# A graph layer on one core: 80 half-target edge buckets in place of 40, chunk addresses loaded four at a time, plain groups out of PSUM by ScalarE, small edge tables partly on GpSimd

## The reference

```python
for r in range(weight.shape[0]):
    mask = (edge_type == r).astype(x.dtype)
    sums = jax.ops.segment_sum(msgs * mask[:, None], dst, num_segments=n)
    cnt = jax.ops.segment_sum(mask, dst, num_segments=n)
    mean = sums / jnp.maximum(cnt, 1.0)[:, None]
    out = out + mean @ weight[r]
```

## Time and profile before

| what | value |
|---|---|
| median of 3 runs | 1880.09 us |
| span of the profiled execution | 1878.8 us |
| PE busy | 1794.9 us (96%) |
| DVE busy | 1023.3 us (54%) |
| ACT busy | 478.5 us (25%) |
| POOL busy | 701.1 us (37%) |
| first stage, start to last histogram add | 0 to 427.5 us |

### The profile page before, as it was taken

How to read it: one execution, slowest core, us unless ns; L and a number is a source line. 1 busy time by engine, 2 the same in 40 slices (tenths; PEclk the granted TensorE clock), 3 DMA queues, 4 the chain that set the end, 5 groups by cost and what they waited for, 6 DMA issues and landing times.

```text
span 1878.8 us, 28666 instructions
## 1 busy us (share of the span) xinstructions
PE 1794.9 (96%) x9953; PEld 1477.4 (79%) x9953; DVE 1023.3 (54%) x2540; ACT 478.5 (25%) x1055; POOL 701.1 (37%) x609
## 2 busy tenths in 40 slices
PE   6999999999999999999999999954999999999999
PEld 4876689987777778787777887742899888878987
DVE  7888999997254543526354356786632224362311
ACT  3139956662010110101011145243100000111100
POOL 2110000003634435353534444200485552345862
PEclk9999999999999999999999999956999999999999
DMA  4532222224213121231313534110354351113322
GB/s 134 154 109 77 73 86 79 75 67 129 91 38 89 45 72 56 66 86 47 94 33 113 172 84 131 45 46 7 96 164 146 104 156 51 37 55 118 90 73 66
DMA packets 129282, 162.23 MB, mean 86 GB/s; under 512 B 14288, under 2 KB 75368, under 8 KB 128922
## 3 DMA queue, kind: packets, MB, share of 16 engines
q1 hardware_dynamic: 100848, 120.93, 21.5%
q10 hardware_dynamic: 22250, 23.53, 4.0%
q0 software_dynamic: 6080, 16.40, 2.9%
HBM read 135.51 MB, written 25.30 MB: 86 GB/s over the span
## 4 chain that ended last, share of the span: by engine, by line
PE 84%; DVE 6%; ACT 6%; issue 1%; DVEq 1%; DMA 1%; POOL 0%; ACTq 0%; SPq 0%
PE ps L367 22%; PE ps L368 22%; PE ps L369 21%; PE ps L1236 9%; PE ps L892 3%; ACT sc_col L838 2%; ACT sc_row L837 1%; PE ps L1201 1%; DVE w_lo L318 1%; PE ps L881 1%; PE ps L1156 1%; DMA nat<-in_x 1%; ACT w_hi L313 1%; PE ps L1183 1%; PE ps L1211 0%
## 5 line engine op out<-in xcount | busy, mean ns | idle before, releaser
L367 PE MATMUL ps<-w_hi,xt_hi 128*125 128x512 f32 x1320 | 539.0, 408 | 9.1 <-DVE xt_lo L549 3.5
L256 POOL TENSOR_TENSOR w_hi<-w_stage,zero 128x512 fp32r<-128x512 f32 x256 | 276.8, 1081 | 684.4 <-PE ps L369 670.0
L368 PE MATMUL ps<-w_lo,xt_hi 128*125 128x512 f32 x1320 | 523.0, 396 | 0.0
L369 PE MATMUL ps<-w_hi,xt_lo 128*125 128x512 f32 x1320 | 521.5, 395 | 0.0
L259 POOL TENSOR_TENSOR w_lo<-w_stage,w_hi 128x512 fp32r<-128x512 f32 x256 | 346.2, 1352 | 20.1
L367 PEld LDWEIGHTS ps<-w_hi,xt_hi 128*125 128x125 f32 x1320 | 246.6, 187 | 67.1 <-DVE xt_lo L549 4.3
L369 PEld LDWEIGHTS ps<-w_hi,xt_lo 128*125 128x125 f32 x1320 | 246.0, 186 | 63.3
L368 PEld LDWEIGHTS ps<-w_lo,xt_hi 128*125 128x125 f32 x1320 | 246.3, 187 | 53.5
L367 PE MATMUL ps<-xt_hi,w_hi 128*128 128x314 f32 x736 | 250.5, 340 | 1.3 <-DVE ring L2430 0.6
L369 PE MATMUL ps<-xt_hi,w_lo 128*128 128x314 f32 x736 | 225.9, 307 | 0.0
L368 PE MATMUL ps<-xt_lo,w_hi 128*128 128x314 f32 x736 | 225.7, 307 | 0.0
(11 more groups left out here) (392 smaller groups left out, 2390.2 us busy)
## 6 DMA issues: line engine op xcount, KB each, us to landing
w_stage<-in_stream SPq DMA_DIRECT2D x374, 256.0 KB, 2.7
pre<-ring POOLq DMA_DIRECT2D x30, 250.0 KB, 3.8
a_qt<-pre_t SPq DMA_DIRECT2D x18, 312.5 KB, 3.8
a_qt<-pre_t ACTq DMA_DIRECT2D x14, 312.5 KB
pre_t<-ring_t POOLq DMA_DIRECT2D x12, 312.5 KB, 2.8
pre_t<-ring_t ACTq DMA_DIRECT2D x12, 312.5 KB
a_vx<-pre SPq DMA_DIRECT2D x9, 312.5 KB
nat<-pre SPq DMA_DIRECT2D x2, 1250.0 KB
```

The source lines that it names most:

```text
L256: POOL.tensor_tensor(w_hi[:, q, :], w_stage[:, q % NST, :], zero[:].to_broadcast([128, 512]), ALU.add).then_inc(S("hi_done"), 1)
L367: PE.matmul(dst, l_hi, r_hi, start=first, stop=False)
L368: PE.matmul(dst, l_hi, r_lo, start=False, stop=False)
L369: return PE.matmul(dst, l_lo, r_hi, start=False, stop=last)
```

## The change

- **Buckets.** The key gets the half of the target (destination at or above 314): 80 buckets (NKEY) of 314 columns. A chunk of 128 edges, not a group of 256, belongs to one bucket; there are still 240 chunks, now 120 pairs. Per pair: 2 matmuls of 314 columns, each into its own bank (banks 4, 5 and 6, 7 in turn), one ACT copy of 2x314, and per chunk one hot column of 314 and one add of 314 int16. Hot rows are made four chunks at once by one tensor_tensor of 128x(128x4), float16. Hot tiles are made 4 chunks ahead (LEAD_HOT), in the order add(c), hot(c + 4), and each add also waits for the add before it. The idle slots of the first turned group are 1, 2 and every fourth from 7 to 35.
- **Addresses.** `g_start` holds each chunk's start in `adj`; four are loaded into registers by one call each four chunks.
- **Edge tables.** Three keys are packed as fields of one number in 28 rows (28x166 = 4648 elements in place of 6600), with one tensor_tensor more (`key_weight`), and later unpacked. GpSimd makes the field weights, a float16 key, and the column and row numbers (some 15 operations of 125x166). The positions' chunk starts are looked up by 80 tensor_scalar of 166 elements (one a key) into `key_start` and five halving adds of int16.
- **Plain groups 0 to 3** leave PSUM by ACT (copy without bias), each ahead of the last chunk split of its group. Their bias is added on DVE once they are read back, 125x2560 an operation: `bias_half(nat, 0)` and `(nat, 1)` around the feed steps of the projection, `bias_half(z, 0)` and `(z, 1)` ahead of the two clips (L1548). Four more transfers (SP) bring these biases.
- POOL's store and split loops stand later in the program's text; their order among themselves is as it was.

```diff
+SPLIT = 314
+NKEY = 2 * NBUCKET
+FIELDS, NROW = 3, 28
+CHUNK = 128
+NCHUNK = (EDGES + NKEY * (CHUNK - 1)) // CHUNK
+NPAIR = NCHUNK // 2
...
+        def evacuate_plain(g):
+            for m in range(T):
+                wait_bank(ALE, g, m, c0, g0)
+                if g:
+                    ALE.wait_ge(S(f"st{tag}_{m}"), 16 * g)
+                ALE.activation(ring[:, m, :], ps[0:P, m, :], ACT.Copy).then_inc(S("bank_free"), 1)
...
+        DVE.tensor_tensor(key_weight[:], key_hot[:], e_weight[:].unsqueeze(1).to_broadcast([P, NROW, EW]), ALU.mult)
...
+    def hist_add(c, start):
+
+        DVE.wait_ge(S("hi_main"), c // 2 + 1)
+        if c:
+            DVE.wait_ge(S("hi_add"), c)
+        o = adj[:, bass.ds(start, SPLIT)]
+        DVE.tensor_tensor(o, o, counts[c // 2 % 4][:, c % 2, :], ALU.add).then_inc(S("hi_add"), 1)
+
+    def hist_pe(g):
+
+        if g >= 2:
+            PE.wait_ge(S("hi_main"), g - 1)
+        if g == 1:
+            PE.wait_ge(S("bank_free"), (SC0 + SC_GROUPS + 1) * T)
         for j in range(2):
+            c = 2 * g + j
+            PE.wait_ge(S("hi_dve"), c + 1)
+            PE.matmul(ps[0:P, pair_bank(g) + j, 0:SPLIT], hot_row[c // 4 % 2][:, 0:P, c % 4], hot_col[c % 8][:],
+                      start=True, stop=True).then_inc(S("hi_pe"), 1)
...
         for g in range(3):
-            load_bias(g)
-            for c in range((g + 1) * KT, (g + 2) * KT):
+            for c in range((g + 1) * KT, (g + 2) * KT - 1):
                 split_act(c)
-        load_bias(3)
+            evacuate_plain(g)
+            split_act((g + 2) * KT - 1)
...
+        starts = dict(enumerate(hist_starts(0)))
         for h in range(HI_GROUPS):
             for n in range(per):
-                g = h * per + n
-                if g + 2 < NGROUP:
-                    hist_dve_hot(g + 2, (g + 2) % 4)
-                if chunk_at(h, n):
-                    split_dve(chunk_at(h, n))
-                if g % 4 == 0:
-                    packed = DVE.value_load(gpack[0:1, g // 4:g // 4 + 1], min_val=0, max_val=2 ** 24 - 1)
-                hist_dve_add(g, g % 4, packed)
+                for c in (2 * (h * per + n), 2 * (h * per + n) + 1):
+                    hist_add(c, starts[c])
+                    if c + LEAD_HOT < NCHUNK:
+                        hist_hot(c + LEAD_HOT)
+                    if c % STARTS == 0 and c + STARTS < NCHUNK:
+                        starts.update(zip(range(c + STARTS, c + 2 * STARTS), hist_starts(c + STARTS)))
+                    if c % 2 == 0 and chunk_at(h, n):
+                        split_dve(chunk_at(h, n))
...
     DVE.tensor_copy(dis[:], rs[:])
+    DVE.wait_ge(S("ld_bh"), 32)
+    bias_half(nat, 0)
     for k in range(5, KT):
         feed_dve(k, k)
+        if k == 6:
+            bias_half(nat, 1)
...
     DVE.drain().then_inc(S("rgam"), 1)
+    DVE.wait_ge(S("ld_z"), 32)
+    DVE.wait_ge(S("ld_bh"), 64)
+    for g in range(2):
+        bias_half(z, g)
     for i, w in enumerate((w1, w2)):
         DVE.wait_ge(S("w_round"), i + 1)
```

More of the change, by code:

```diff
@@ L498, in dense @@
                 dense_pe(g, c0, g0, between=between)
-        side(dense, evacuate, evacuate_half, load_bias)
+        side(dense, evacuate_plain, evacuate, evacuate_half, load_bias)
         stored(groups - 2)
@@ L727, in bucket_counts @@
-        evacuate(0)
+        DVE.scalar_tensor_tensor(e_key[:], e_key[:], 2.0, e_half[:], ALU.mult, ALU.add)
+        DVE.drain()
+        row, first = e_row[:, 0:EC], e_first[:, 0:EC]
+        DVE.tensor_scalar(first, e_key[:], float(NROW), None, ALU.is_ge)
+        DVE.tensor_scalar(e_second[:], e_key[:], float(2 * NROW), None, ALU.is_ge)
+        edge_tables(sig(DVE.drain(), "dve_step"))
+        DVE.scalar_tensor_tensor(row, first, -float(NROW), e_key[:], ALU.mult, ALU.add)
+        DVE.drain()
@@ L895, in beside, with pair_bank, hist_hot @@
-    def beside(dense, evacuate, evacuate_half, load_bias):
-        mk = bucket_counts(evacuate)
+    LEAD_HOT, STARTS = 4, 4
+    def pair_bank(g):
+        return 4 if g % 2 else 6
+    def hist_hot(c):
+        if c % 4 == 0:
+            if c >= 8:
+                DVE.wait_ge(S("hi_pe"), c - 4)
+            DVE.tensor_tensor(hot_row[c // 4 % 2][:], iota1_by4[:],
+                              slot_row[:, c:c + 4].unsqueeze(1).to_broadcast([128, 128, 4]), ALU.is_equal)
+        if c >= 8:
+            DVE.wait_ge(S("hi_pe"), c - 7)
+        DVE.tensor_scalar(hot_col[c % 8][:], iota1_16[:, 0:SPLIT], slot_col[:, bass.ds(c, 1)], None,
+                          ALU.is_equal).then_inc(S("hi_dve"), 1)
@@ new lines, in hist_copy, with hist_starts @@
+    def hist_copy(g):
+        b = pair_bank(g)
+        ALE.wait_ge(S("hi_pe"), 2 * g + 2)
+        if g >= 4:
+            ALE.wait_ge(S("hi_add"), 2 * g - 6)
+        ALE.activation(counts[g % 4][:], ps[0:P, b:b + 2, 0:SPLIT], ACT.Copy).then_inc(S("hi_main"), 1)
+    def hist_starts(c):
+        top = (NBUCKET - 1) * NB + SPLIT
+        return nc.values_load_multi_w_load_instructions(
+            g_start[0:1, c:c + STARTS], engines=(mybir.EngineType.DVE,), min_val=0, max_val=top,
+            skip_runtime_bounds_check_because="a bucket's number is below NKEY")[1]
@@ L975, in beside, with idle @@
                 DVE.wait_ge(S("sc_pe"), sc_per + EC + 1)
[L976 removed]
+                DVE.tensor_copy(slot_col[:], slot_ps[:, 0:NCHUNK])
+                DVE.tensor_copy(slot_row[:], slot_ps[:, NCHUNK:2 * NCHUNK])
                 DVE.drain()
[L978 to L979 removed]
+                for c in range(LEAD_HOT):
+                    hist_hot(c)
             evacuate(i + SC0)
[L982 to L983 removed]
         HI0 = SC0 + SC_GROUPS
         assert HI0 + HI_GROUPS == G_PRE0
[L986 to L987 removed]
+        per = NPAIR // HI_GROUPS
+        assert per * HI_GROUPS == NPAIR and per * 4 == KT * T * 3
+        def idle(h, s_):
+            return s_ in (1, 2) or s_ > 2 and s_ % 4 == 3 and 3 < s_ < 36 if h == 0 else s_ % (4 if h < HI_GROUPS - 1 else 8) == (
+                3 if h < HI_GROUPS - 1 else 7)
         def hist_of(h, s_):
[L990 to L992 removed]
+            n = sum(not idle(h, i) for i in range(s_))
+            return n if not idle(h, s_) and n < per else None
         def first_step(h, k):
@@ L1093, in build, with load_bias_h @@
     load_rounds(C_REL + 2 * NSL, C_PROJ - NSL, KT * G_PROJ)
+    def load_bias_h(row):
+        for g in range(2):
+            r = B_PRE0 + row + g
+            SP.dma_start(bias_h[g][:], a["bias"][r:r + 1, :].rearrange("o (k f) -> o k f", k=4).to_broadcast([P, 4, 128])).then_inc(S("ld_bh"), 16)
     def sp_late(c):
```

355 lines of the change are left out of this document (190 added, 165 removed).

## The result

The changed kernel takes 1885.35 us, the median of ten runs (1882.55 to 1887.32); the kernel before took 1879.99 in ten runs beside it (1879.24 to 1880.39). The ratio is 1.0028, with a 95% interval of 1.0019 to 1.0037. It is slower by 5.4 us, where I had forecast 1.0 us faster, a change too small to be measured. The time lies in the stated range. The spread of the changed kernel is four times that of the kernel before.

What follows compares the result with a forecast made beforehand. The histogram was taken as bound by DVE and PE together. Tables 0.8, before the histogram -0.4, projection biases 0, histogram -5.0 and z biases 3.6 gave -1.0: 1879.1 us, own range 1872 to 1886, with rivals 1858 to 1893.

Steps and rivals of the forecast that it cites:

- tables, to the first scatter tile: Edge tables: DVE's end covered, but ACT evacuates group 3 behind zeroing `adj`; +0.8 us, bounds -0.5 and +6.
- from there to the first add: Before the histogram: DVE makes the first four hot tiles in 1.2 for 1.84, copies slots in two steps; -0.4 us.
- first add to the end: Histogram: a column group takes 44.2 us against 45.8, one more window at the end +1.4; -5.0 us in all.
- gate, z biases: Gate: two bias operations run from 1139.0 to 1144.6 ahead of the clips, which start 3.6 late without cover; +3.6 us.
- upper bound of +5.6: Gate: the most that the z biases were taken to cost, in us; the lower bound was 0.
- rival 1: Histogram: latency is hidden and the loop goes by its load, 38.3 to 42 a group; 1850 to 1866 us, chance 0.26.
- address loads: Histogram on DVE: loading four addresses takes 0.13 us each time, x 7.5 = 1.0 a column group; 0 to 0.6 possible.
- 32 us of idle time before the adds: Histogram on DVE: idle time before the add's line, about 0.27 a pair, ended by ACT's copy.
- Rival 2: Histogram: the loop is slower than before, add waiting for ACT's copy, 49 a group; 1891 to 1897 us, chance 0.16.
- Rival 3: Edge tables: 80 lookups at 0.3 make them late, PE stands around 100 to 130 us; 1884 to 1888, chance 0.10.
- Rival 4: Gate: the z biases cost nothing because their transfers are early; -3.6, 1875.5 us, chance 0.08.
- the signs: Forecast wrong if a histogram column group is under 43 or over 46 us, or if PE stands before 140 us.

Runs made afterwards that it cites:

- x3_b2: The kernel before with two operations of 125x2560 on z (its maximum with itself) ahead of the clips, without bias transfers: 1883.93 us.
- x1_early: The changed kernel with the two z bias transfers issued by SP five chunks earlier: 1884.35 us.
- x8_static: The changed kernel with each add at a fixed address and no address loads (counts go to wrong buckets): 1878.90 us, one run.
- x9_nochain: As x8_static, but each add waits for the add 8 chunks before, not for the last one: 1876.13 us, one run.
- x6_ev3: The changed kernel with the z biases moved behind the clips and group 3 taken out of PSUM by DVE, lead 4: 1871.44 us, one run.
- x7_lead6: As x6_ev3, with hot tiles made 6 chunks ahead of their add, not 4: 1863.75 us.
- x11_lead8: As x7_lead6, with a lead of 8 chunks, 12 hot columns and three tiles of hot rows: 1859.13 us.
- x4_b4: The kernel before with four operations of 125x2560 on z ahead of the clips: 1890.20 us.

## Why the prediction was wrong

Step by step, profile against profile:

| step | forecast | measured |
|---|---|---|
| tables, to the first scatter tile | +0.8 | +1.7 (143.50 for 141.82) |
| from there to the first add | -0.4 | -2.0 (101.80 for 103.81) |
| first add to the end | -5.0 | -3.6 (178.25 for 181.84) |
| gate, z biases | +3.6 | +10.3 (stand 8.8, clock 1.5) |
| all else (projection -0.3, the rest behind the gate) | 0 | +0.7 |
| sum | -1.0 | +7.1 in the profile, +5.4 by the medians |

The first row is uncertain by some 1.2 us, the spread of that mark over profiles with the same tables. The second and third belong together. In the kernel before, four hot tiles and a split (243.92 to 245.63) stood in front of the first add; now the add comes ahead of them, so the mark itself has moved. Together -5.4 was forecast and -5.6 measured.

**The step that failed** is the last of the sum, "the later lands 22.1 after its issue, at 1138.2; the bias transfers, issued behind the weight stream, land about then or later. So the biases run from 1139.0". The mechanism was wrong, not only the size: I let z set the start, and made the lower end of an open bound ("then or later") into the term. z landed 20.8 us after its issue, at about 1133, but the bias transfers, which SP issues in order behind the first weight chunks of the gate, were issued only at 1131.91 and 1132.29 and had landed at 1141.08. Counted from the end of the first stage, which was 3.9 earlier, the biases started 6 us later than forecast, and DVE's wait of 12.20 was ended by them. The upper bound of +5.6 was wrong in the same way: it took the biases' length as the most that they can cost, though the wait in front of them had no bound.

Two more things were missing. A PE that stands this long is granted 1.2 GHz at first afterwards (1.5 us). And I priced the move on DVE alone: x3_b2 shows that DVE's additions beside GpSimd's `w_lo` stretch both. In the changed kernel itself this did not act, since the biases came when GpSimd was through. With earlier operations it acts: it makes nearly all of the 3.8 us of x3_b2, and a part of the 9.5 of x1_early (1884.35 - 1874.84), where the larger part is late weights.

**The histogram was right**, in kind and nearly in size: 44.4 us a column group in the middle for 44.2, 46.5 in the first, and the add waits for ACT's copy of a pair whose hot tiles were made too late. The runs with leads of 6 and 8 show the cause, and that rival 1 was only an edit away: 42.4 and 40.7 us a group, and with the other edits 1863.75 and 1859.13 us, inside its 1850 to 1866. But one term was worked out wrongly. Thirty pairs are 15 times four chunks, not 7.5, so the address loads at my price were 2.0 us and the group 45.2 (and the upper bound 4.5 more than 49.9). That this is the average of the three distances (the kernel before has 46.2 by the same count) is partly luck: x8_static prices loads and register addresses together at 1.3. And I expected 32 us of idle time before the adds; it was 17.4. Part of the rest hides in distances, as this timeline of DVE in the changed kernel shows:

```profile
321.40 0.33 DVE L957 TENSOR_TENSOR adj<-adj,counts 125x314 int16 x1
321.64 0.42 DVE L929 TENSOR_TENSOR hot_row<-iota_by,slot_row 128x512 f16<-128x512 f16 x1
321.97 0.30 DVE L933 TENSOR_SCALAR hot_col<-iota,slot_col 128x314 f16<-128x314 f16 x1
322.19 0.32 DVE L957 TENSOR_TENSOR adj<-adj,counts 125x314 int16 x1
322.42 0.30 DVE L933 TENSOR_SCALAR hot_col<-iota,slot_col 128x314 f16<-128x314 f16 x1
322.74 0.33 DVE L957 TENSOR_TENSOR adj<-adj,counts 125x314 int16 x1
```

Where the add before is close, a hot tile is followed by the next add after 0.32 (322.42 to 322.74; 0.28 in most such places), not 0.22, and no idle time is shown; the adds stand 0.55 apart. x8_static and x9_nochain show whose price this is: 0.21 with fixed addresses, with the chain and without it. My sum had no term for an address in a register, only for its loading.

**Rival 2** (slower by the loop) had the sign of the result with another cause; its place was faster than before. **Rival 3** (late tables) did not come: the lookups of 166 elements stood 0.18 us apart (41 in 7.21 us), at the low end of 0.17 to 0.30, and DVE waited 6.39 us for ACT's `w_hi` before the scatter. **Rival 4** had the transfers early; they were late. Of the signs, no column group was under 43 us, and the three distances are 46.5, 44.4 and 44.6, so the first is over the 46 that I had set, in a count in which the kernel before has 45.8 there; PE's waits before 140 us are those of the kernel before within 0.3 us in sum.

Of the rule on the fixed extra per instruction (the Trainium skill, "VectorE: DVE Perf Modes", the section on the TRN2 errata) this trace shows a part: two adds of 314 take 0.321 busy each for 0.480 of one of 626. The four-row hot tile starts 0.33 ahead of its successor (321.64, 321.97), where I had 0.34; the same page of the Trainium skill, in its section on what auto-detection checks, has 16-bit operands with step 1 move two at a time, and the trace agrees with that.

## What to carry to other kernels

Work that is moved to an idle stretch costs what it waits for, not what it is long: look up when its operands land, and which transfers stand in front of theirs, before calling the stretch free. Moving a transfer forward has a price too, for it then stands in front of others (x1_early). Then look at who shares it: a GpSimd that splits weights beside a VectorE that adds in SBUF slows both. And when an engine's load falls, the lead between producer and consumer, counted in time, falls with it; here, from first to last add, the histogram took 177.4 us with a lead of four chunks, 166.8 with six and 160.9 with eight (x6_ev3, x7_lead6, x11_lead8).

## What the runs showed of the hardware

- GpSimd's `w_lo` (128x512, float32) takes 1.28 to 1.30 us alone and up to 3.84 beside VectorE's 125x2560 float32 additions in SBUF; VectorE's clip of 128x2048 takes 1.23 alone and 2.2 to 2.3 beside GpSimd (x3_b2, x1_early), its second addition 3.89 for 2.82 (x1_early).
- PE's granted clock fell to 0.50 (1.2 GHz) during a stand of 9.16 us and was 1.00 again about 3.3 us after its end; it fell in the stands of 5.34 (x4_b4) and 5.65 us (x1_early) too. After stands of 2.1 to 2.5 us at this place (x3_b2, x4_b4) it stayed 1.00.
- An add whose address stands in a register starts about 0.07 us later behind a hot tile than one with a fixed address (0.28 for 0.21). With fixed addresses a wait for VectorE's own add before, with one operation between, costs nothing (x8_static, x9_nochain).
- Two transfers that each spread 2 KB over 125 partitions (250 KB), issued beside the weight stream, landed 9 us after their issue. Much of that is the stretch: the 256 KB weight chunks issued at 1133 to 1137 us took 7.8 (median), where the median over the whole program is 2.7.
